# A perceiver-style block of four attention layers: the third layer's MLP in high and low parts

## The chip, the cores and the metric

The kernel runs on one core of one Trainium2 chip (trn2). The core has five engines that run their own queues of instructions in order: TensorE (PE in the profile; PEld is its weight load), VectorE (DVE), ScalarE (ACT), GpSimd (POOL) and SyncE (SP), which issues most DMAs. They meet through semaphores. The metric is the device time in microseconds (us); the number that counts is the median of several executions.

## The reference, cut to what matters

`x` has 8 batches of 256 rows of 256 values, `ctx_2048` 8 x 64 rows. Four layers follow one another, each on the whole output of the last; all arithmetic is fp32.

```python
x = _L0_xattn_ref(x, ctx, mask, ...)   # norm of ctx, 16 heads of 16, gated residual
x = _L1_xattn_ref(x, ctx, mask, ...)   # 32 heads of 8, 8 groups, residual, then a norm
x = _L2_xattn_ref(x, ctx, mask, ...)   # below: attention and MLP
x = _L3_xattn_ref(x, ctx, ctx, ...)    # two attentions with 16 heads of 128, then an MLP

def _L2_xattn_ref(...):                # the third layer
    ...                                # norm, q, k, v, softmax over 64 keys, 16 heads
    hidden = out + residual            # out @ cproj_w + cproj_b
    residual = hidden
    y = layer_norm(hidden, ln2_w, ln2_b)
    y = jax.nn.gelu(y @ fc_w + fc_b, approximate=True)   # 256 -> 1024
    y = y @ proj_w + proj_b                              # 1024 -> 256
    return residual + y
```

In the fourth layer the keys get a bias row and the MLP uses the exact gelu; before it, `kh = kv_in @ wk + bk` and `vh = kv_in @ wv + bv` project the context.

## The kernel before, in words

**Units.** The first three layers' attentions are cut into 24 units, one for each layer and batch (`NU` = 24; u = 0 to 7, 8 to 15 and 16 to 23). A unit of the third layer has two tiles of 128 rows. Each engine's program is one loop over u with a row of calls in fixed order, written out by hand; iteration u holds several units' stages: the scores of unit u, the source and queries of units u + 2 and u + 1, and the output of unit u - 1. Iteration 24 closes the last unit. Nothing is scheduled dynamically: an engine stands at a wait until it is met.

**TensorE** in an iteration of the third layer: scores of the first tile (L537), `source` (four transposes of the normed input, L421), values and keys, transposes of the previous unit's late tile (`probs_transposed`, L546), scores of the second tile, `reciprocals_transposed` (L560), `weighted` (L579), transposes of this unit's first tile, queries, `output` (L595). In iteration u, `source` needs the norm of unit u + 2 from ScalarE, and its bank is free when VectorE's `unit_residual` has added the output of unit u - 2, which stands at the head of VectorE's iteration u.

**VectorE**: `unit_residual` (L1076), sums and reciprocals of the unit before (L1050, L1057), maximum (L1028), shift (L1044) and statistics (L962, L966) of a tile, `unit_normal` (L1063), `tile_sums` (L1050). **ScalarE**: exponentials and the transposed tiles' copies (L1495, L1502), `unit_queries` (L1434), and last in the iteration the norm of a coming unit (`ln_finish`, L1484). **GpSimd**: `key_diagonal` (L1757), `reciprocals_spread` (L1769), `unit_bias` (L1797) and, for each tile, `tile_sums` (L1779, L1782), which folds the exponentials into halves and quarters for VectorE's sum; `rstd` (L1738, L1741) raises a variance to -1/2 for a norm.

**The third layer's MLP** comes behind the loop, in blocks b = 0 to 7 (one batch each). On TensorE: `mlp_source` (four transposes of the normed block), `hidden` (four banks f of 2 x 2 fp32 matmuls 128x256, L709), `projected` (16 matmuls, L722), where two banks of block b stand ahead of `projected(b - 1)` and two behind it. ScalarE applies bias and gelu (L1613). VectorE does the norm (`mlp_norm`), the affine out of PSUM (`mlp_source`, L978), the residual (`mlp_residual`, L1198); GpSimd `rstd` and the bias row on `x` (`add_row`, L1791). Between them VectorE prepares the fourth layer's weights: `wq_sums` (L1221), `wq_biased` (L1235) and `value_sums`.

**Parts.** The fourth layer's MLP is computed in products of parts already. An fp32 value is split into a high part, ScalarE's copy into the type fp32r, and a low part, VectorE's subtraction of it. `products` issues three matmuls of parts (high x high, high x low, low x high; L899 to L901) for one of fp32. The weights are split with `weight_high` (L1679) and `weight_low` (L1342), the source and the hidden values in every block (`hidden_low`, L1391; `last_hidden` on ScalarE, L1720).

**Memory and loads.** `w3` holds the small layers' weights and then four regions of the fourth layer's (queries, keys, values, output projection); `pair[0]` and `pair[1]` hold the context, the third layer's MLP weights (`w_fc`, `w_pr`) and hidden buffers. SyncE loads the fourth layer's weights (`load_w3`, L396) once the last unit's residual is done. **The fourth layer's start**: steps j from -4 on; `key_projection` (16 matmuls, L745) waits at i = 0 for the last MLP residual, at i = 1 for a bank.

## Time and profile before

| what | value |
|---|---|
| median of 3 runs (lowest, highest) | 1135.33 us (1134.01, 1136.47) |
| the profiled execution | 1134.86 us, span 1133.1 us |
| mean granted TensorE clock, share of full speed | 0.982 |
| TensorE busy | 1050.7 us, 93% |
| VectorE, ScalarE, GpSimd busy | 56%, 43%, 35% |
| chain that ended last | PE 79%, ACT 7%, POOL 7%, issue 4%, DVE 3% |
| DMA over the span | 27 GB/s |
| fourth layer's value weights | 8 DMAs of 512.0 KB, 7.7 us from issue to landing |

The span is the profiled part of one execution; the busy share of an engine is its busy time over the span. The chain is followed back from the last instruction, at each step to what released it. Rows below have the form: line in the kernel, engine, operation, output<-inputs, shape, count, and in brackets the idle time before it with what ended it. TensorE's fp32 matmuls leave two records each.

### The profile page before, as it was taken

To read this page: it belongs to the slowest core of one execution; us is meant where nothing else is said; L and a number is where in the kernel's file an instruction comes from. 1 tells how busy PE (TensorE), PEld (TensorE's weight loads), DVE (VectorE), ACT (ScalarE), POOL (GpSimd) and SP (SyncE) were. 2 spreads that over 40 slices of the span, in tenths; PEclk is the share of its full clock that TensorE was granted. 3 is DMA by queue.
4 is the path that set the end of the run, shared out by engine and by line. 5 is a ranking of instruction groups with operands and counts; after the bars stand their busy time and mean duration, and the time that the engine had idled before them with its cause. 6 is when DMAs were issued, how large, how long until landed. Compare 5 with 4: busy or idle time off the path is not lost.

```text
span 1133.1 us, 17012 instructions
## 1 busy us (share of the span) xinstructions
PE 1050.7 (93%) x6780; PEld 814.2 (72%) x6780; DVE 629.5 (56%) x1079; ACT 491.6 (43%) x988; POOL 400.5 (35%) x416
## 2 busy tenths in 40 slices
PE   6999889887899799989999999999999999978997
PEld 3666555555576688878777777777777777648997
DVE  3657888778577323732444555765444445473552
ACT  2556777676676222214333333233332333224543
POOL 2534578688975312310222212332111221231230
PEclk9999999998999999999999999999999999988999
DMA  9000000000000620000000022310000001000000
GB/s 309 33 2 1 1 1 1 1 1 1 1 1 1 223 93 1 1 1 1 1 1 1 1 75 79 108 38 1 1 1 1 1 1 64 12 0 1 29 20 29
DMA packets 17043, 32.22 MB, mean 28 GB/s; under 512 B 3522, under 2 KB 8388, under 8 KB 16452
## 3 DMA queue, kind: packets, MB, share of 16 engines
q1 hardware_dynamic: 16964, 31.13, 8.0%
q8 instruction: 54, 0.88, 0.3%
q14 instruction: 25, 0.20, 0.1%
HBM read 29.03 MB, written 2.10 MB: 27 GB/s over the span
## 4 chain that ended last, share of the span: by engine, by line
PE 79%; ACT 7%; POOL 7%; issue 4%; DVE 3%; DMA 0%; POOLq 0%; DVEq 0%; ACTq 0%
PE work L745 10%; PE work L857 10%; PE scores L796 9%; PE work L813 5%; PE scores L709 5%; PE work L722 5%; PE work L846 4%; PE work L546 4%; PE work L503 3%; PE work L595 3%; PE work L421 2%; PE work L579 2%; PE scores L537 2%; PE work L828 2%; POOL pair L1779 2%
## 5 line engine op out<-in xcount | busy, mean ns | idle before, releaser
L857 PE MATMUL work<-pair,probsT 128*128 128x256 f32 x512 | 123.5, 396 | 11.0 <-ACT pair L1658 8.8
L857 PEld LDWEIGHTS work<-pair,probsT 128*128 128x128 f32 x512 | 97.9, 196 | 36.3 <-issue 20.3
L1738 POOL TENSOR_SCALAR stat<-stat 128x2 f32<-128x2 f32 (+1 forms) x49 | 11.2, 228 | 318.4 <-DVE stat L966 317.1
L745 PE MATMUL work<-ctxT,w 128*128 128x128 f32 x1024 | 120.2, 275 | 3.5 <-ACT pair L1649 1.6
L745 PEld LDWEIGHTS work<-ctxT,w 128*128 128x128 f32 x1024 | 118.2, 192 | 5.2 <-issue 3.1
L796 PE MATMUL scores<-pair,act_bufs 128*128 128x512 f32 x256 | 115.2, 592 | 0.0
L1649 ACT ACTIVATE pair<-work 128x512 f32<-128x512 f32 x64 | 38.2, 598 | 154.3 <-PE work L813 154.3
L1639 ACT ACTIVATE kvT<-work,cols 128x128 f32<-128x128 f32 x128 | 36.6, 369 | 154.5 <-PE work L745 154.5
L1880 POOL TENSOR_TENSOR probs<-probs,smax 128x1024 f32<-128x1024 f32 x22 | 42.0, 1909 | 159.2 <-DVE smax L1314 159.2
L1294 DVE TENSOR_REDUCE smax<-scores 128x16 f32<-128x1024 f32 x32 | 39.2, 1225 | 77.1 <-PE scores L796 77.1
L796 PEld LDWEIGHTS scores<-pair,act_bufs 128*128 128x128 f32 x256 | 46.4, 190 | 46.0 <-issue 45.9
L1285 DVE TENSOR_TENSOR kvT<-work,cols 128x512 f32<-128x512 f32 x32 | 22.1, 691 | 94.0 <-PE work L745 94.0
L813 PEld LDWEIGHTS work<-kvT,w 128*128 128x128 f32 x512 | 61.9, 192 | 16.4 <-issue 16.4
L1028 DVE TENSOR_REDUCE smax<-scores 128x16 f32<-128x1024 f32 x48 | 57.8, 1205 | 21.4 <-PE scores L537 20.8
L1613 ACT ACTIVATE pair<-scores,cols 128x256 f32<-128x256 f32 x64 | 26.9, 471 | 88.6 <-PE scores L709 88.6
L813 PE MATMUL work<-kvT,w 128*128 128x128 f32 x512 | 62.5, 275 | 2.6 <-ACT kvT L1639 2.6
L846 PE MATMUL work<-w,kvT 128*64 128x256 f32 x512 | 62.3, 385 | 0.0
L722 PE MATMUL work<-pair 128*128 128x256 f32 x256 | 56.7, 379 | 0.9 <-ACT pair L1613 0.9
L546 PEld LDWEIGHTS work<-ident,pair 128*128 128x128 f32 x256 | 29.4, 148 | 38.1 <-ACT pair L1495 27.2
L546 PE MATMUL work<-ident,pair 128*128 128x128 f32 x256 | 37.3, 292 | 20.0 <-ACT w L1502 11.9
L722 PEld LDWEIGHTS work<-pair 128*128 128x128 f32 x256 | 48.6, 190 | 7.9 <-ACT pair L1613 1.3
L1791 POOL TENSOR_TENSOR x<-x,rows_late 128x512 f32<-128x512 f32 x32 | 49.7, 1552 | 12.5 <-DVE act_bufs L972 9.9
(174 smaller groups left out, 2398.3 us busy)
## 6 DMA issues: line engine op xcount, KB each, us to landing
w<-in_l_wk SPq DMA_DIRECT2D x8, 512.0 KB, 6.3
w<-in_l_wq SPq DMA_DIRECT2D x8, 512.0 KB, 7.0
w<-in_l_wv SPq DMA_DIRECT2D x8, 512.0 KB, 7.7
w<-in_l_wo SPq DMA_DIRECT2D x8, 512.0 KB, 8.4
out<-x SPq DMA_DIRECT2D x8, 256.0 KB, 2.2
x<-in_x SPq DMA_DIRECT2D x1, 1536.0 KB, 9.2
pair<-in_l_fc SPq DMA_DIRECT2D x1, 1024.0 KB, 7.2
pair<-in_l_pr SPq DMA_DIRECT2D x1, 1024.0 KB, 9.2
```

The costliest lines, as they stand in the source:

```text
L546: last = tr(work[half][:, q * P:(q + 1) * P], probs[k % 4][:, (4 * half + q) * P:(4 * half + q + 1) * P], ident[:, :])
L709: last = mm(fbank[f][:, j * T:(j + 1) * T], w_fc[:, c, (2 * f + j) * P:(2 * f + j + 1) * P], srcT[(NU + b) % 3][:, c, :], start=(c == 0), ...
L722: last = mm(work[b % 2][:, t * D:(t + 1) * D], hid_bufs[b % 2][:, f, t * P:(t + 1) * P], w_pr[:, f, :], start=(f == 0), stop=(f == FC - 1))
L745: last = mm(bank[:, h * P:(h + 1) * P], w[:, c, (4 * g + h) * K3:(4 * g + h + 1) * K3], ctxT[:, c, p * P:(p + 1) * P], start=(c == 0), sto ...
L796: last = mm(sc[j % 2][:, half * BANK:(half + 1) * BANK], fixed[j // 2 % 2][:, c, t * P:(t + 1) * P], pk[n % 2][:, bb, c, half * BANK:(half ...
L813: last = mm(step_banks(j)[2 + c][:, h * P:(h + 1) * P], w3_wq[:, 4 * g + h, c * P:(c + 1) * P], kvT[i % 2][:, h, :], start=True, stop=True)
L846: last = mm(bank[h * S:(h + 1) * S, bb * D:(bb + 1) * D], kvT[2][:, 2 * q + h, bb * S:(bb + 1) * S], w3_wo[:, 4 * g + 2 * q + h, :], start ...
L857: last = mm(step_banks(j + 1)[0][:, 0:D], probsT_bufs[j % 2][:, q, :], pv[n % 2][:, bb, q, :], start=(q == 0), stop=(q == GH // 2 - 1))
L1028: v.tensor_reduce(smax[k % 2][:, 0:GH], s3, X, ALU.max).then_inc(d_max, 1)
L1294: v.tensor_reduce(m, s3, X, ALU.max).then_inc(d_lmax, 1)
L1791: g.tensor_tensor(xb(b), xb(b), row(name).unsqueeze(1).broadcast_to([P, TT, D]), ALU.add).then_inc(done, 1)
L1880: g.tensor_tensor(pr, pr, smax[j % 2][:, 32:48].unsqueeze(2).broadcast_to([P, H3, S]), ALU.mult).then_inc(p_pr, 1)
```

## The change

The third layer's MLP goes over to three products of parts. Its weights are split in pieces (`mlp_pieces`), one in each of the iterations u = 17 to 24: the high part at the end of ScalarE's iteration, the low one near the end of VectorE's. Statistics, norm, `rstd` and bias row of blocks 0 to 2 move from behind the loop into iterations 21 to 23, the block's source into iteration 24, and `hidden(0, 0)` too, ahead of the last unit's `output`. In each block VectorE now makes the low part of the source and four low parts of the hidden values, ScalarE their high parts. `mlp_norm` of a block runs three blocks ahead instead of two. The parts need room: the fourth layer's value weights move to the first region of `w3`, and are loaded when the MLP's last product is done. The fourth layer's second key projection follows the first one directly, in a bank of the scores.

```diff
-        w_fc, w_pr = cut(DC, F), cut(FC, D)
+        mlp_raw = cut(2, DC * F)
...
-        w3_wq = w3[:, 0:WN].rearrange("p (h d) -> p h d", h=H3)
+        w3_wv = w3[:, 0:WN].rearrange("p (c n) -> p c n", c=DC)
...
+        m2_w1 = parts_at("m2_w1", w3_at, DC, F, step=pair_at[1] - w3_at)
+        m2_w2 = parts_at("m2_w2", w3_at + n_w, FC, D, step=pair_at[1] - w3_at)
+        m2_hid = [parts_at(f"m2_hid{i}", pair_at[0] + 2 * i * n_hid, FC, T) for i in range(2)]
...
+        def key_bank(i):
+            return fbank[0] if i == 1 else step_banks(i - 4)[0]
...
+        def mlp_pieces(u):
+            return {17: [0], 18: [1], 19: [2], 20: [3], 21: [4], 22: [5], 23: [6], 24: [7]}.get(u, [])
...
-                load_w3(1, g, "kqvo")
+                load_w3(1, g, "kqo")
+            e.wait_ge(pe_f2, B)
+            for g in range(4):
+                load_w3(1, g, "v")
...
+            def products(bank, stationary, moving, start, stop):
+                (s_hi, s_lo), (m_hi, m_lo) = stationary, moving
+                mm(bank, s_hi, m_hi, start=start, stop=False)
+                mm(bank, s_hi, m_lo, start=False, stop=False)
+                return mm(bank, s_lo, m_hi, start=False, stop=stop)
+            def mlp_source(b):
+                e.wait_ge(*NORMS["m2", b])
+                if b == 0:
+                    e.wait_ge(d_seen, NK)
+                elif b == 1:
+                    e.wait_ge(a_rT, NU)
+                elif b == 2:
+                    e.wait_ge(d_res, NU)
+                else:
+                    e.wait_ge(d_mT, 2 * (b - 2) + 2)
+                transposes(fbank[3] if b == 0 else work[2 + b % 2], norm[(B + b) % 3]).then_inc(pe_mx, 1)
+            def hidden(b, f):
+                e.wait_ge(a_sh, b + 1)
+                e.wait_ge(d_sl, b + 1)
+                e.wait_ge(a_wh, 4)
+                e.wait_ge(d_wl, 4)
...
+                for j in range(2):
+                    for c in range(DC):
+                        last = products(fbank[f][:, j * T:(j + 1) * T],
+                                        [w[:, c, (2 * f + j) * P:(2 * f + j + 1) * P] for w in m2_w1],
+                                        [v[:, c, :] for v in m2_src[b % 2]], c == 0, c == DC - 1)
+                last.then_inc(pe_f1, 1)
+            def projected(b):
+                e.wait_ge(a_hh, 4 * b + 4)
+                e.wait_ge(d_hl, 4 * b + 4)
+                e.wait_ge(a_wh, 8)
+                e.wait_ge(d_wl, 8)
...
+                        last = products(work[b % 2][:, t * D:(t + 1) * D],
+                                        [v[:, f, t * P:(t + 1) * P] for v in m2_hid[b % 2]],
+                                        [w[:, f, :] for w in m2_w2], f == 0, f == FC - 1)
+                last.then_inc(pe_f2, 1)
...
+                    if u == NU:
+                        mlp_source(0)
                     for k in late:
                         probs_transposed(k)
...
                     if u > 0:
                         reciprocals_transposed(u - 1)
                         weighted(u - 1)
+                    if u == NU:
+                        hidden(0, 0)
...
                 if u > 0:
                     output(u - 1)
...
-                        last = mm(fbank[f][:, j * T:(j + 1) * T], w_fc[:, c, (2 * f + j) * P:(2 * f + j + 1) * P],
-                                  srcT[(NU + b) % 3][:, c, :], start=(c == 0), stop=(c == DC - 1))
...
-            mlp_source(0, False)
-            for b in range(B + 1):
+            for f in range(1, 4):
+                hidden(0, f)
+                if f == 1:
+                    mlp_source(1)
+            for b in range(1, B + 1):
...
+                if i == 1:
+                    e.wait_ge(a_g, 4 * B)
+                else:
+                    first_free(j)
+                project(w3_wk, i, key_bank(i)).then_inc(pe_kp, 1)
...
-                if key is not None:
+                if key is not None and key != 1:
                     key_projection(j, key)
+                if key == 0:
+                    key_projection(j + 1, 1)
...
+            def mlp_stats(b):
+                e.wait_ge(d_res, 2 * B + b + 1)
+                ln_stats(("m2", b), xb(b), TT)
+            def mlp_norm(b):
...
+                ln_finish(("m2", b), xb(b), norm[(B + b) % 3], TT)
+            def mlp_weight_low(q):
+                w, q = divmod(q, 4)
+                n = mlp_raw.shape[2] // 4
+                high, low = (flat(v)[:, q * n:(q + 1) * n] for v in (m2_w1, m2_w2)[w])
+                e.wait_ge(a_wh, 4 * w + q + 1)
+                v.tensor_tensor(low, mlp_raw[:, w, q * n:(q + 1) * n], high.bitcast(F32), ALU.subtract).then_inc(d_wl, 1)
+            def mlp_source(b):
...
+                affine(fbank[3] if b == 0 else work[2 + b % 2], srcT[i % 3], "l2_g2", "l2_b2", d_mT)
+                e.wait_ge(a_sh, b + 1)
+                e.wait_ge(d_mT, 2 * b + 2)
+                v.tensor_tensor(m2_src[b % 2][1], srcT[i % 3], m2_src[b % 2][0].bitcast(F32), ALU.subtract).then_inc(d_sl, 1)
+            def mlp_hidden_low(b, f):
+                e.wait_ge(a_hh, 4 * b + f + 1)
+                high, low = (p[:, 2 * f:2 * f + 2, :] for p in m2_hid[b % 2])
+                v.tensor_tensor(low, m2_whole[f], high.bitcast(F32), ALU.subtract).then_inc(d_hl, 1)
...
+                if NU - 3 <= u < NU:
+                    mlp_stats(u - NU + 3)
+                for q in mlp_pieces(u):
+                    mlp_weight_low(q)
+                if NU - 3 <= u < NU:
+                    mlp_norm(u - NU + 3)
...
-            mlp_norm(0)
-            mlp_source(0)
-            mlp_norm(1)
             for b in range(B + 1):
+                for f in range(2):
+                    if b < B:
+                        mlp_hidden_low(b, f)
+                if b + 1 < B:
+                    mlp_source(b + 1)
                 if b > 0:
                     mlp_residual(b - 1)
-                if b + 1 < B:
-                    mlp_source(b + 1)
-                if b + 2 < B:
-                    mlp_norm(b + 2)
+                for f in range(2, 4):
+                    if b < B:
+                        mlp_hidden_low(b, f)
+                if b + 3 < B:
+                    mlp_stats(b + 3)
+                    mlp_norm(b + 3)
...
+            def mlp_weight_high(q):
+                w, q = divmod(q, 4)
+                n = mlp_raw.shape[2] // 4
+                e.wait_ge(s_in["l2_fc" if w == 0 else "l2_pr"], 16)
+                e.wait_ge(pe_wo, 2 * B)
+                act(flat((m2_w1, m2_w2)[w][0])[:, q * n:(q + 1) * n], mlp_raw[:, w, q * n:(q + 1) * n],
+                    ACT.Copy).then_inc(a_wh, 1)
+            def mlp_source_high(b):
+                e.wait_ge(d_mT, 2 * b + 2)
+                if b < 2:
+                    e.wait_ge(pe_rT, NU)
+                    e.wait_ge(d_rec, NU)
+                else:
+                    e.wait_ge(pe_f1, 4 * (b - 2) + 4)
+                    e.wait_ge(d_sl, b - 1)
+                act(m2_src[b % 2][0], srcT[(NU + b) % 3], ACT.Copy).then_inc(a_sh, 1)
...
+                for q in mlp_pieces(u):
+                    mlp_weight_high(q)
...
+            def mlp_hidden(b, f):
                 e.wait_ge(pe_f1, 4 * b + f + 1)
...
+                for j in range(2):
+                    last = act(m2_whole[f][:, j, :], fbank[f][:, j * T:(j + 1) * T], ACT.Gelu_apprx_tanh,
+                               bias=col("l2_fcb", 2 * f + j))
+                last.then_inc(a_g, 1)
+                e.wait_ge(a_g, 4 * b + f + 1)
+                if b >= 2:
                     e.wait_ge(pe_f2, b - 1)
-                for j in range(2):
-                    last = act(hid_bufs[b % 2][:, 2 * f + j, :], fbank[f][:, j * T:(j + 1) * T], ACT.Gelu_apprx_tanh,
-                               bias=col("l2_fcb", 2 * f + j))
-                last.then_inc(a_h, 1)
+                act(m2_hid[b % 2][0][:, 2 * f:2 * f + 2, :], m2_whole[f], ACT.Copy).then_inc(a_hh, 1)
...
+            def mlp_bias(b):
+                e.wait_ge(*NORMS["m2", b])
+                e.wait_ge(s_in["rows_late"], 16)
+                add_row(b, "l2_pb", p_xm)
...
+                if NU - 3 <= u < NU:
+                    rstd(("m2", u - NU + 3), TT)
+                    mlp_bias(u - NU + 3)
...
-            for b in range(B):
+            for b in range(3, B):
                 rstd(("m2", b), TT)
-                e.wait_ge(*NORMS["m2", b])
-                add_row(b, "l2_pb", p_xm)
-                if b >= 6:
-                    wq_scaled(1, b - 6)
-            wq_scaled(1, 2)
-            wq_scaled(1, 3)
+                mlp_bias(b)
+            for q in range(4):
+                wq_scaled(1, q)
```

The name of a buffer in the rows that follow is shortened by the listing (`m_w_high` is a part of the MLP's weights, `m_src_high` one of its source; `w` and `pair` are the two large regions).

**GpSimd, iterations 21 and 22**, from the second tile of unit 20 on. Before:

```order
L1779 TENSOR_TENSOR pair<-pair 128x512
L1782 TENSOR_TENSOR pair<-pair 128x256
L1779 TENSOR_TENSOR pair<-pair 128x512
L1782 TENSOR_TENSOR pair<-pair 128x256
L1769 COPY pair<-recs 128x512
L1791 TENSOR_TENSOR x<-x,pair 128x512
```

After:

```order
L1882 TENSOR_TENSOR pair<-pair 128x512
L1885 TENSOR_TENSOR pair<-pair 128x256
L1841 TENSOR_SCALAR stat<-stat 128x2
L1844 TENSOR_TENSOR stat<-stat,minus_half 128x2
L1894 TENSOR_TENSOR x<-x,rows_late 128x512
L1882 TENSOR_TENSOR pair<-pair 128x512
L1885 TENSOR_TENSOR pair<-pair 128x256
L1872 COPY pair<-recs 128x512
L1894 TENSOR_TENSOR x<-x,pair 128x512
```

Between the two `tile_sums` (one pair of rows L1779, L1782 for each tile) now stand `rstd` and the bias row of MLP block 0, which is the row ending in `rows_late`; the same stands in iterations 22 and 23.

**VectorE, the end of an iteration** (in 16 to 18), `unit_normal`, `tile_sums`, and the next iteration's `unit_residual`. Before:

```order
L1063 TENSOR_TENSOR pair<-work,pair 128x512
L1050 TENSOR_REDUCE sums<-pair 128x16
L1076 TENSOR_TENSOR x<-work,x 128x512
L1050 TENSOR_REDUCE sums<-pair 128x16
L1057 RECIPROCAL recs<-sums 128x32
L1028 TENSOR_REDUCE smax<-scores 128x16
```

After:

```order
L1104 TENSOR_TENSOR pair<-work,pair 128x512
L1091 TENSOR_REDUCE sums<-pair 128x16
L1160 TENSOR_TENSOR m_w_low<-pair,m_w_high 128x512
L1117 TENSOR_TENSOR x<-work,x 128x512
L1091 TENSOR_REDUCE sums<-pair 128x16
L1098 RECIPROCAL recs<-sums 128x32
L1069 TENSOR_REDUCE smax<-scores 128x16
```

The subtraction of a weight piece stands ahead of the residual `x<-work,x`.

**TensorE, the last unit and the MLP's start.** Before:

```order
L546 MATMUL work<-ident,pair 128x128 x8
L560 MATMUL work<-ident,pair 128x128 x4
L579 MATMUL work<-w,pair 32x256 x8
L595 MATMUL work<-w,pair 128x256 x4
L421 MATMUL work<-ident,pair 128x128 x4
L709 MATMUL scores<-act_bufs,pair 128x256 x8
L421 MATMUL work<-ident,act_bufs 128x128 x4
```

After:

```order
L609 MATMUL work<-w,pair 128x256 x4
L435 MATMUL scores<-ident,pair 128x128 x4
L560 MATMUL work<-ident,pair 128x128 x8
L574 MATMUL work<-ident,pair 128x128 x4
L593 MATMUL work<-w,pair 32x256 x8
L630 MATMUL scores<-m_src_high,m_w_high 128x256
L631 MATMUL scores<-m_src_low,m_w_high 128x256
L632 MATMUL scores<-m_src_high,m_w_low 128x256
```

The source's transposes stood behind the last `output` (L595); now they stand ahead of the last late tile's transposes (L435 after), and the first bank of `hidden` follows `weighted` (L593) directly.

## Rows read from the trace of the kernel before

**Rows 1.** Stretches of all engines: start:end, length, busy us per engine, clock, DMA, GB/s.

```profile
255.00:270.00 15.00, 11.62 (x82) 7.72 (x80) 14.69 (x24) 10.87 (x21) 12.37 (x15) 0.89 0.01 1
345.00:360.00 15.00, 15.00 (x118) 11.19 (x111) 9.74 (x13) 9.45 (x17) 8.61 (x9) 1.00 0.00 0
```

**Rows 2.** Timeline of TensorE, third layer's MLP: start, length (us), the instruction.

```profile
382.09 5.32 PE L709 MATMUL scores<-act_bufs,pair 128*128 128x256 f32 x16 [1.09 <-DVE act_bufs L978]
...
491.56 7.17 PE L722 MATMUL work<-pair 128*128 128x256 f32 x32 [0.93 <-ACT pair L1613]
```

**Rows 3.** Timeline, fourth layer's MLP.

```profile
1036.44 0.36 PE L899 MATMUL scores<-src_high,w_high 128*128 128x256 f32 x1 [1.35 <-ACT src_high L1704]
...
1057.74 1.00 DVE L978 TENSOR_SCALAR act_bufs<-work,cols 128x256 f32<-128x256 f32 x2 [2.81 <-PE work L421]
...
1062.22 0.69 DVE L1391 TENSOR_TENSOR hid_low<-w,hid_high 128x512 fp32r<-128x512 f32 x1 [0.70 <-ACT hid_high L1720]
...
1069.69 1.00 DVE L978 TENSOR_SCALAR act_bufs<-work,cols 128x256 f32<-128x256 f32 x2 [2.81 <-PE work L421]
...
1129.78 0.69 DVE L1198 TENSOR_TENSOR x<-work,x 128x512 f32<-128x512 f32 x1 [7.62 <-PE work L901]
```

**Rows 4.** Timeline, the last unit.

```profile
368.60 1.27 POOL L1779 TENSOR_TENSOR pair<-pair 128x512 f32<-128x512 f32 x1 [0.67 <-ACT pair L1495]
...
372.25 0.66 PE L560 MATMUL work<-ident,pair 128*128 128x128 f32 x4 [1.75 <-POOL pair L1769]
```

**Rows 5.** Timeline of VectorE, the weights' sums in the third layer's MLP.

```profile
487.82 1.22 DVE L1221 TENSOR_TENSOR w<-w,pair 128x1024 f32<-128x1024 f32 x1
...
490.58 4.01 DVE L1235 SCALAR_TENSOR_TENSOR pair<-w,cols,pair 128x256 f32<-128x256 f32 x4
```

**Rows 6.** Timeline, the fourth layer's weights split.

```profile
998.56 1.13 ACT L1679 ACTIVATE w_high<-w 128x512 fp32r<-128x512 f32 x2
...
1000.49 1.90 POOL L1880 TENSOR_TENSOR probs<-probs,smax 128x1024 f32<-128x1024 f32 x1 [11.94 <-DVE smax L1314]
...
1000.60 4.01 DVE L1342 TENSOR_TENSOR w_low<-w,w_high 128x512 fp32r<-128x512 f32 x2
```

**Rows 7.** Timeline, two boundaries of units, around TensorE's source transposes.

```profile
307.23 0.63 PE L421 MATMUL work<-ident,act_bufs 128*128 128x128 f32 x4 [1.57 <-ACT act_bufs L1484]
...
338.31 1.08 ACT L1484 ACTIVATE act_bufs<-x,stat 128x256 f32<-128x256 f32 x2
...
339.31 0.69 DVE L1076 TENSOR_TENSOR x<-work,x 128x512 f32<-128x512 f32 x1 [2.65 <-PE work L595]
...
339.63 1.04 POOL L1757 TENSOR_TENSOR w<-w,pair 128x512 f32<-128x512 f32 x1
...
340.38 0.66 PE L421 MATMUL work<-ident,act_bufs 128*128 128x128 f32 x4
```

**Rows 8.** Timeline, third layer's MLP, a block's norm and bias row.

```profile
388.80 0.74 DVE L962 BATCH_NORM_STATS2 stat<-x 128x6 f32<-128x256 f32 x2
...
391.72 1.27 POOL L1791 TENSOR_TENSOR x<-x,rows_late 128x512 f32<-128x512 f32 x1 [0.85 <-DVE act_bufs L972]
```

**Rows 9.** Timeline, the end of iteration 21 and the next one's start.

```profile
348.64 0.84 ACT L1434 ACTIVATE pair<-work,cols 128x256 f32<-128x256 f32 x2
...
348.65 1.28 POOL L1779 TENSOR_TENSOR pair<-pair 128x512 f32<-128x512 f32 x1 [1.69 <-ACT pair L1495]
...
351.69 1.16 DVE L1028 TENSOR_REDUCE smax<-scores 128x16 f32<-128x1024 f32 x1
...
354.14 1.06 ACT L1495 ACTIVATE probs<-probs 128x1024 f32<-128x1024 f32 x1
...
356.26 1.09 PE L546 MATMUL work<-ident,probs 128*128 128x128 f32 x8
```

**Rows 10.** Timeline of TensorE, first and third key projection of the fourth layer.

```profile
499.61 2.02 PE L745 MATMUL work<-ctxT,w 128*128 128x128 f32 x16 [0.88 <-DVE x L1198]
...
511.91 3.81 PE L745 MATMUL work<-ctxT,w 128*128 128x128 f32 x32 [0.78 <-ACT pair L1649]
```

198 lines of the change are left out of this document (86 added, 112 removed).

## The prediction

> **What bounds the kernel now.** I first read the page: TensorE is busy 93% of the span, no other engine over 56%, and the chain of work that ended last is TensorE's to 79%. An average hides stages, so I then read stretches. Around 345 to 360 us, in the later units of the third layer, TensorE is busy all 15.00 us while VectorE, ScalarE and GpSimd have 5 to 6 us free each; around 255 to 270 us it is busy only 11.62 [rows 1]. Then the timeline of the MLP that is changed. Here TensorE works without a gap from 382.09 us to 498.73: 32 records of fp32 128x256 take 7.17 us, and each full matmul leaves two records, so one costs some 0.43 us [rows 2]. Last, the fourth layer's MLP, which already does the same arithmetic in high and low parts, as a ruler: a block every 1069.69 - 1057.74 = 11.95 us for 96 products and 4 transposes (0.12 us a product, 0.36 for three) and, from its second block's first product at 1036.44 to the last residual at 1129.78, 93.3 us [rows 3].
>
> I count the units as the loop does, u = 16 to 23 for the third layer, and "iteration 24" closes it.
>
> **1. The MLP itself.** Removed: 256 fp32 matmuls; added: 768 products. Before, from the last unit's transposed reciprocals (372.25) to the MLP's first matmul are 9.84 us, and to its end 116.6 more: 126.5 in all [rows 2, 4]. After: the source's affine lies ready, so behind those reciprocals come ScalarE's copy out, its high part, VectorE's low part, some 2.6 us; then on TensorE 48 products (5.8), the last unit's output, which now stands among them (2.0), and transposes (0.4). TensorE has just idled, and before the first 16 records took 5.32 us where 32 take 7.17 [rows 2]: 1.7 to 1.9 us of slow start, which I keep. The second block waits about 1.4 for its low source, since the first residual and first hidden parts stand ahead of it. That is 14.0 us, then the ruler's 93.3.
>
> VectorE has more to do here than in the fourth layer's MLP. From the start of `wq_biased` to the end of `value_sums` are 494.59 - 487.82 = 6.8 us [rows 5], once a block in the last four blocks. In the ruler VectorE's chain from affine (1057.74) to the end of the block's last low part (1062.22, 0.69 long) is 5.1 us, as it waits for ScalarE in between, and two low parts (1.3) come before the next affine [rows 3]. With the 6.8 this is 13.2 us against TensorE's 11.95. In block 4 the 5.6 (no `wq_biased`) come on top of block 7's norm, with GpSimd's row held against it: the affine comes 3.7 us late, 0.4 of it slack. The next block adds 1.2. So 3.3 + 1.2 = 4.6 us. Sum: 14.0 + 93.3 + 4.6 = 111.9 against 126.5: **-14.6**. Bounds: without any VectorE lateness -19.2; with all of blocks 1 to 7 paced by VectorE at 13.2 to 13.6, -7.5.
>
> The Trainium skill ("FP8 and Floating Point Precision", TensorE Precision Notes) counts true fp32 as four passes, high by high, high by low, low by high and low by low. By passes alone three products would take 3/4 of the time, 0.32 instead of 0.36, and the MLP would save another 256 x 0.04 = 10 us. The ruler's row gives 0.12 a product [rows 3], and I go by it.
>
> **2. Splitting the weights in units 17 to 24.** Eight copies on ScalarE, two take 1.13 us, and eight subtractions on VectorE. Two of these, with both inputs in SBUF, take 4.01 us where GpSimd works at 1000.49, instead of 1.3: the first one finds GpSimd's 1.90 us running and ends after it [rows 6]. Busy time is no argument against them, VectorE has 5 us free; their place is. ScalarE copies at the end of its unit, and VectorE's subtraction, at the end of its own, waits for that copy; behind it in VectorE's queue stands `unit_residual`, and for this TensorE's `source` waits. Before, at 339.31: ScalarE's norm ends at 339.39, the residual runs at once, TensorE transposes at 340.38 [rows 7]. After: copy to 340.0, then GpSimd's `key_diagonal` (339.63, 1.04 us) is in the way to 340.7, subtraction to 341.3, residual to 341.95, transposes at 342.0: 1.6 us late, TensorE having nothing else in its queue. So at the starts of iterations 19, 20, 21: 3 x 1.6. At the start of 18 the norm itself is late (TensorE waits 1.57 us for it and starts at 307.23) and the same sequence ends at 309.25: 2.0 [rows 7]. Later units have no source. Sum **+6.8**. TensorE is full there, so nothing gives it back. Bounds: 3.0 (0.5 to 1.0 each, if ScalarE comes earlier), 9.
>
> **3. Norms and rows of blocks 0 to 2 in units 21 to 23.** They leave the stretch after the last unit (counted in 1) and pay at the end of each unit. The price is on GpSimd: its queue now has `rstd` and `mlp_bias`, with `tile_sums` of the unit's second tile behind them. `mlp_bias` waits for VectorE's norm, this for the subtraction, this for ScalarE's copy, this for `unit_queries` (to 349.48). From the statistics to GpSimd's row are 391.72 - 388.80 = 2.9 us where nothing is between [rows 8]. In unit 21 the statistics are done before the copy, which ends at 350.05; subtraction to 350.7, norm to 351.35, row to 352.75 [rows 9]. `tile_sums` starts then, not at 348.65, 4.1 us late. From it to the reciprocals' transposes are 3.65 us (368.60 to 372.25), and maximum, shift and exponentials take 3.5 (351.69 to 355.20) from a start 2.8 after it [rows 4, 9]: exponentials end at 359.0, transposes at 359.05 instead of 356.26. **2.8** for this unit. Played through in the same way, unit 22 adds 3.8 (its first-tile transposes come 6.6 late) and unit 23 another 3.7, since each time the second `tile_sums` stands behind three waits of other engines: the last reciprocals come 10.3 us later than at 372.25: **+10.3**. Bounds: 4 (the row costs its 1.27 alone, three times) and 13.
>
> **4. The end of the MLP and the fourth layer's start.** `value_sums` of group 3 stands ahead of the last residual: it starts some 0.8 late and the first key projection waits for it: **+0.8**. The second key projection now follows the first directly, in a scores bank. Before, from the first (499.61) to the third (511.91) are 12.3 us, TensorE waiting for ScalarE between the products [rows 10]; now the first key bias hides beside the second projection, about 10.4: **-1.9** (0 to -2.5). The values' weights are issued when the MLP's last product is done, four DMAs; they are wanted 12 us later. I cost them at nothing; that cover is gone if 512 KB took over 12 us.
>
> Everything later moves as a whole.
>
> **Sum:** -14.6 + 6.8 + 10.3 + 0.8 - 1.9 = +1.4 us. The profiled execution took 1134.86 (span 1133.1), so 1136.3; the median of the runs shown is 0.5 above that execution: **1136.7 us**. A measurement of this kernel tells 0.2%, 2.3 us, from no change: the bounds are 1133.1 and 1137.6.
>
> **Rivals.**
> A. The waits at the units' ends are mostly hidden. For it: all three engines have over 4 us free per 15 [rows 1], and a shift in one unit can be caught by another. Against: in iterations 19 to 21 TensorE has no gap to catch it with. Price: term 2 at 3.4, term 3 at 7, VectorE's lateness at 2.6: -16.6 + 3.4 + 7 + 0.8 - 1.9 = -7.3, 1128.0 us.
> B. VectorE paces the whole MLP. Place: `hidden_low` and `mlp_source` on its queue. It decides as soon as its work and its waits for ScalarE pass 11.95 us in a block; with statistics and norm (2.9 with the wait for GpSimd), four low parts and the source it is at 9.2 already without the weights' sums, so one more us in a handoff of each kind would do it. Price: the upper bound of term 1, +7.1 on my sum: 1143.8 us. A low clock in units 22 to 24 works in the same direction: at 255 to 270 us, busy 11.62 of 15, the granted clock is 0.89 [rows 1], and these units fall to a like share. The skill ("TensorE: Matmul & The Clock Gate", The HAM clock gate) says that the throttled state is the default and activity lifts it, which speaks against this change; 0 to 3 us by the row.
> C. Three of four passes. By the passes' rule (named in 1) the MLP saves another 10 us: 1126.5. The row at 0.12 us speaks against it.
>
> **Chances.** My forecast 0.34 (own range 1133.5 to 1140), A 0.31, B 0.33, C 0.02. Of my forecast's 0.34 about 0.25 lies within 0.2%, 0.02 below and 0.07 above. Faster 0.31 + 0.02 + 0.02 = 0.35, same 0.25, slower 0.33 + 0.07 = 0.40. Range 1127 to 1144: it takes in A's and B's centres.
>
> **What would show it.** In the changed profile: (1) TensorE 0.12 us apart in the third layer's MLP, blocks at 11.95 us early, 13 or more in blocks 5 and 6, with VectorE without gaps; (2) TensorE's four source transposes of units 20 to 23 each waiting 1.5 to 2 us for VectorE's residual, and subtractions of 1.2 us or more; (3) GpSimd's first `tile_sums` of a new unit 4 us after its exponentials in 22 to 24; (4) third key projection some 10.4 us after the first. I am wrong if the last unit ends less than 10 us later than before, or if the MLP's blocks stay at 11.95 throughout.

## The result: 0.36% slower, and where the profile after shows it

| | before | after |
|---|---|---|
| median of 20 executions | 1135.21 us (1133.97 to 1137.16) | 1139.34 us (1136.14 to 1143.41) |
| ratio, 95% interval | | 1.0036 (1.0023 to 1.0048) |
| profiled execution | 1134.86 us, span 1133.1 | 1136.14 us, span 1134.0 |
| mean granted clock | 0.982 | 0.979 |
| TensorE busy | 1050.7 us, 93% | 1035.2 us, 91% |

The forecast was 1136.7 us. The 20 times after fall into two groups, ten of 1136.1 to 1138.6 us with a mean clock of 0.979 to 0.974 and ten of 1140.1 to 1143.4 with 0.973 to 0.971. The profiled execution is the fastest of all. So between the two profiled executions stand 1.3 us of the 4.1; the rest goes together with a lower mean clock, to which the experiments come back.

TensorE in the profile after, at the places of [rows 2, 4, 7, 10] (start, length, instruction, idle time before it and its releaser):

```profile
309.71 0.66 PE L435 MATMUL work<-ident,act_bufs 128*128 128x128 f32 x4 [3.51 <-DVE x L1117]
...
323.84 0.66 PE L435 MATMUL work<-ident,pair 128*128 128x128 f32 x4 [1.42 <-DVE x L1117]
...
348.95 0.66 PE L435 MATMUL work<-ident,act_bufs 128*128 128x128 f32 x4 [1.42 <-DVE x L1117]
...
391.43 0.66 PE L574 MATMUL work<-ident,pair 128*128 128x128 f32 x4 [3.66 <-POOL pair L1872]
...
394.06 0.36 PE L630 MATMUL scores<-m_src_high,m_w_high 128*128 128x256 f32 x1 [0.98 <-ACT m_src_high L1609]
...
406.78 0.55 PE L630 MATMUL scores<-m_src_high,m_w_high 128*128 128x256 f32 x1 [4.58 <-ACT m_src_high L1609]
...
464.72 0.60 PE L435 MATMUL work<-ident,pair 128*128 128x128 f32 x4
...
481.64 0.60 PE L435 MATMUL work<-ident,act_bufs 128*128 128x128 f32 x4
...
507.25 2.02 PE L774 MATMUL work<-ctxT,w 128*128 128x128 f32 x16 [0.87 <-DVE x L1264]
509.11 1.95 PE L774 MATMUL scores<-ctxT,w 128*128 128x128 f32 x16
...
517.46 3.81 PE L774 MATMUL work<-ctxT,w 128*128 128x128 f32 x32 [0.78 <-ACT pair L1752]
```

The first three rows, and one at 336.40 us with 1.43 that is left out, are the last four source transposes: they wait for VectorE's residual. The reciprocals' transposes of the last unit stand at 391.43 us where they stood at 372.25, the first key projection at 507.25 instead of 499.61, the third at 517.46 instead of 511.91. As a ledger: +19.2 before the MLP, -11.5 in it, -2.1 in the key projections, so +5.55 at the third key projection; from there to the end 616.54 us instead of 621.19, -4.65, though the instructions there are the same.

The same two stretches as in [rows 1], and one in the MLP (start:end, length, busy PE, PEld, DVE, ACT, POOL, granted clock, DMA share, GB/s):

```profile
255.00:270.00 15.00, 11.60 (x80) 7.09 (x77) 14.31 (x23) 10.23 (x20) 12.46 (x14) 0.89 0.00 0
345.00:360.00 15.00, 13.58 (x101) 9.56 (x99) 10.50 (x18) 9.61 (x19) 7.51 (x9) 1.00 0.01 1
...
469.00:481.00 12.00, 9.56 (x67) 9.59 (x68) 10.40 (x21) 6.29 (x13) 2.58 (x1) 0.86 0.00 1
```

TensorE, full at 345 to 360 us before, now has 1.4 us of gaps there, and in the MLP a stretch with 2.4 us of gaps and the clock at 0.86: part of it ran at the lower level, 1.2 GHz, after TensorE had waited 3.25 us (until 471.44).

### The profile page after: what moved, and what is told of

The parts are those of the page before. It is cut to its first block, busy times and chain, and to the rows that moved or that the text cites. A ratio compares the mean times of both kernels' runs of the same rounds, so it can differ in the third digit from the quotient of the medians.

```text
span 1134.0 us, 17672 instructions
## 1 busy us (share of the span) xinstructions
PE 1035.2 (91%) x7036; PEld 811.9 (72%) x7036; DVE 662.4 (58%) x1127; ACT 518.1 (46%) x1036; POOL 403.4 (36%) x416
## 4 chain that ended last, share of the span: by engine, by line
PE 72%; ACT 8%; POOL 8%; DVE 6%; issue 5%; DMA 1%; POOLq 0%; DVEq 0%; ACTq 0%
PE work L774 10%; PE work L890 10%; PE scores L829 9%; PE work L846 5%; PE work L879 4%; PE work L560 3%; PE work L630 3%; PE work L631 3%; PE work L632 3%; PE work L517 2%; PE scores L630 2%; PE scores L631 2%; PE scores L632 2%; POOL pair L1882 2%; PE work L435 2%
## 5 line engine op out<-in xcount | busy, mean ns | idle before, releaser
L890 PE MATMUL work<-pair,probsT 128*128 128x256 f32 x512 | 120.3, 388 | 11.0 <-ACT pair L1761 8.8
L1572 ACT ACTIVATE w<-work 128x512 f32<-128x512 f32 x88 | 47.7, 593 | 14.3 <-PE work L560 14.2
L1013 DVE TENSOR_SCALAR act_bufs<-x,stat 128x256 f32<-128x256 f32 x58 | 43.2, 787 | 14.9 <-POOL stat L1844 14.9
L1882 POOL TENSOR_TENSOR pair<-probs 128x512 f32<-128x512 f32 x32 | 40.8, 1276 | 29.4 <-ACT probs L1565 29.2
```

Of the source, the lines that this page charges most:

```text
L890: last = mm(step_banks(j + 1)[0][:, 0:D], probsT_bufs[j % 2][:, q, :], pv[n % 2][:, bb, q, :], start=(q == 0), stop=(q == GH // 2 - 1))
L1882: g.tensor_tensor(halves, e3[:, :, 0:n], e3[:, :, n:S], ALU.add).then_inc(p_half, 1)
```

## The experiments

The theory after reading both traces: the loss lies in VectorE's residual behind the weight pieces, GpSimd's rows ahead of its tile sums and, not forecast, a wait for a DMA in VectorE's queue; the first gives most. The rival: these waits take each other's place, and what decides the time is how often TensorE falls to its lower clock.

All ratios and intervals are against the kernel before on the same chip (its medians there lie between 1135.0 and 1136.0 us). Since clock and noise move single executions, each kernel's profile is also read at three places. These hold noise too: after, a1, a3 and b4 run the same code up to the last reciprocals and have them at 390.2 to 393.5 us, so a difference of under 3 us in the first two columns says little by itself.

| kernel | last reciprocals | third key projection | from there to the end | median, ratio (95%) |
|---|---|---|---|---|
| before | 372.25 | 511.91 | 621.19 | 1135.21 |
| after | 391.43 | 517.46 | 616.54 | 1139.34, 1.0036 (1.0023 to 1.0048) |
| a1, after again | 390.37 | 517.89 | 616.91 | 1136.73, 1.0014 (1.0004 to 1.0023) |
| a2 | 382.44 | 508.58 | 616.62 | 1132.19, 0.9971 (0.9949 to 0.9993) |
| a3 | 390.22 | 514.47 | 616.43 | 1134.89, 1.0000 (0.9990 to 1.0009) |
| a4 | 386.05 | 514.48 | 621.12 | 1137.73, 1.0017 (1.0007 to 1.0027) |
| b1 | 378.89 | 503.16 | 616.84 | 1121.15, 0.9871 (0.9856 to 0.9885) |
| b2 | 380.47 | 504.01 | 616.99 | 1125.65, 0.9908 (0.9891 to 0.9925) |
| b3 | 374.52 | 511.96 | 616.44 | 1129.07, 0.9938 (0.9921 to 0.9955) |
| b4 | 393.50 | 517.56 | 620.84 | 1137.90, 1.0021 (1.0009 to 1.0033) |
| c1 | 373.23 | 518.33 | 619.37 | 1139.10, 1.0029 (1.0018 to 1.0041) |
| c2 | 372.21 | 513.53 | 619.27 | 1135.56, 1.0004 (0.9994 to 1.0013) |
| c3 | 378.07 | 498.31 | 616.79 | 1121.96, 0.9893 (0.9846 to 0.9939) |
| d1 | 374.26 | 496.14 | 616.76 | 1114.71, 0.9815 (0.9801 to 0.9828) |

**a1_again.** No edit.

> The changed kernel, unchanged. Its 20 executions lie in two groups, 1136.1 to 1138.6 us with a mean granted clock of 0.974 to 0.979 and 1140.1 to 1143.4 with 0.971 to 0.973, while the 20 of the kernel before lie within 1134.0 to 1137.2. Theory: the upper group is the same program with one or two more stretches at the lower clock, in the third layer's MLP or the units before it, where TensorE now idles more. Rival: the stretch lies in the fourth layer, where nothing was changed, and is chance. The profile shows in which stretches the granted clock is under 1; both theories expect about 1139 us and the same two groups.

Measured: 1136.73 us, all ten executions between 1135.9 and 1138.4 (0.979 to 0.974), so the upper group did not come on this chip, and no profile of the changed kernel holds it. The first theory placed the second group in the MLP and the units, the rival in the fourth layer; this run decides nothing.

**a2_low_behind_residual.** VectorE's subtractions of the weight pieces (`mlp_weight_low`) go behind the next iteration's residual:

```diff
                     tile_shifted(*tiles[0])
...
+                for q in mlp_pieces(u - 1):
+                    mlp_weight_low(q)
...
-                for q in mlp_pieces(u):
-                    mlp_weight_low(q)
```

> VectorE's subtraction of a weight piece goes behind the next iteration's residual and first tile's shift; nothing is left out. Theory: TensorE's waits of 1.4 us for the residual at the source transposes of iterations 19, 20 and 21 and 1.9 of the 3.5 in 18 vanish, and in 21 to 23 the norm no longer stands behind the subtraction and its wait for ScalarE's copy, so GpSimd's row comes 1 to 2 us earlier: last unit's transposed reciprocals 7 to 10 us earlier than 391.4 us, time 6 to 8 us less than the changed kernel. Rival: the subtraction at the new place delays the exponentials by as much, and 0 to 2 us are left.

Measured: the four waits are gone (the source transposes of iteration 18 wait 1.55 us for ScalarE's norm, as before), last reciprocals 7.9 us earlier than in a1, third key projection 9.3. The lowest executions took 1127.2 us against 1135.9; five of ten lie at 1135.0 to 1135.6 with 0.973 to 0.974, so the median fell by 4.5 only, where 6 to 8 were expected. The theory holds for the mechanism and for its price on the path. One part of it does not: the norms no longer stand behind the subtraction, but from the source transposes of unit 23 to the last reciprocals it still takes 42.18 us (42.78 in a1), so GpSimd's row gained nothing to speak of.

**a3_rows_later.**

```diff
-            e.wait_ge(s_in["ln_rows"], 16)
-            for a in range(2):
...
             for b in range(B + 1):
...
+                if b == 1:
+                    e.wait_ge(s_in["ln_rows"], 16)
...
```

> The difference of the fourth layer's norm rows, for which VectorE stands at a DMA until 402.4 us in the changed kernel, goes from ahead of the MLP's first low parts to behind block 1; nothing is left out. Theory: the wait of 4.6 us for the second block's source falls to 1.4 and the time by 3 us. Rival: VectorE, which paces the last blocks with the weights' sums, gives the gain back there: under 1 us.

Measured: the wait falls from 4.54 us to 2.67, the third key projection comes 3.4 us earlier, the lowest execution is 1133.1 against 1135.9, the median 1.8 less. This was the theory, but for the wait, which was to fall to 1.4: 2.67 us are not the DMA's. The row of after that gave the theory is VectorE's, idle for a DMA with the first low parts behind it:

```profile
402.42 0.76 DVE L1306 TENSOR_TENSOR pair<-pair 128x256 f32<-128x256 f32 x2 [4.23 <-DMA pair<-in_ln_rows]
403.10 1.29 DVE L1177 TENSOR_TENSOR m_hid_low<-pair,m_hid_high 128x512 fp32r<-128x512 f32 x2
```

**a4_bias_later.** GpSimd's `mlp_bias(b)` one iteration back, behind `tile_sums(tiles[0][0])`:

```diff
+                if NU - 3 < u <= NU:
+                    mlp_bias(u - NU + 2)
...
                     rstd(("m2", u - NU + 3), TT)
-                    mlp_bias(u - NU + 3)
```

> GpSimd's bias rows of blocks 0 to 2 go one iteration back, behind the tile sums of the next iteration, so that no tile sum stands behind a row that waits for ScalarE's copy, VectorE's subtraction and its norm; rstd stays. Theory (the row's waits cost 10.3 us by the end of the last unit): last reciprocals 7 to 9 us earlier, time 6 to 9 us less. Rival: the row costs only its 1.27 us three times, which stay: under 3 us.

Measured: last reciprocals 4.3 us earlier than in a1, third key projection 3.4; the median is not lower (1137.73), because from there to the end it took 621.12 us instead of 616.91. On the path that is half of the expected 7 to 9 us, between the theory and the rival (under 3); in the median nothing is left of it.

**b1_three_moves.** The three edits together.

> The three moves of the first set together: the subtraction behind the residual, the rows' difference behind block 1, GpSimd's bias rows one iteration back. Fast executions so far: 1136.0 us unchanged, 1127.2, 1133.1 and 1133.6 with one move each. Theory: each removes a wait of its own, but the first took part of the row's wait already (norms no longer stand behind the subtraction), so 8.8 + 2.9 + 1 to 2: fast executions at 1122 to 1124 us, last reciprocals at about 378 us. Rival: what the moves give, the clock takes back, since TensorE stands idle in the same places: a spread of 8 us between executions as with the first move alone, and a median not under 1130.

Measured: 1121.15 us, 15.6 less than a1 and 1.3% under the kernel before; lowest 1120.5; last reciprocals 378.89. The rival said not under 1130 and falls. At the third key projection the three moves add up: 9.3, 3.4 and 3.4 us one by one, 14.7 together. The medians do not (4.5 and 1.8 less, 1.0 more), since the single moves' executions spread over the clock and these four do not.

**b2_sums_spread, b4_spread_alone.** In the kernel before, L1221 is `wq_biased` and L1235 `value_sums` (`wq_sums` stands ahead of them). Of these sums, the value heads go two at a time ahead of the source's affine, on b1 and on the changed kernel:

```diff
+                if 1 <= b < B:
+                    value_heads(1, 2 * b - 2, 2 * b)
                 if b + 1 < B:
                     mlp_source(b + 1)
...
-                    value_sums(1, b - 4)
+                if b == B:
+                    value_heads(1, 14, 16)
```

> As b1_three_moves, and of the fourth layer's weights' sums the 16 value heads go two at a time into blocks 1 to 8 of the MLP, ahead of the source's affine, where VectorE idles 2.8 us at 450.6 in the changed kernel, instead of four at a time in blocks 4 to 7. Theory (VectorE paces blocks 4 to 7: 16.9, 13.3 and 13.0 us instead of 11.95): all blocks at 12 to 12.4, 5 to 6 us less than b1. Rival: the affine is now late in every block, since 2.0 us of heads run against GpSimd's row on the shared port or against ScalarE: each of seven blocks 0.5 to 1 us longer, and no gain.

> The changed kernel with the value heads' spreading of b2 alone. Theory: the block of 16.9 us and the two of 13 go, 5 to 6 us less than the changed kernel's 1136.0 in fast executions, and fewer low-clock stretches at 470 and 495 us, since TensorE no longer idles there: the slow group goes down too. Rival: under 2 us less, as the lateness is ScalarE's (its hidden parts) and not the sums'.

Measured: no gain in the time of either: b2's median is 4.5 us above b1's, b4's 1137.90 lies between the changed kernel's two, 1136.73 and 1139.34. The early blocks stay at 11.95 us, so the rival of b2 (every block longer) is wrong too. The long block takes 16.20 us (451.92 to 468.12) in b2 and 14.70 in b4, where b1 and the changed kernel have 16.92. TensorE's wait in it is 2.52 us in both, where it was 3.25: spreading the heads took 0.7 off. The rest of the difference is the clock, 0.71 behind this wait in b2 (460 to 464 us) and 1.00 in b4. What holds the wait at 2.52, is in b2's timeline:

```profile
451.13 3.48 DVE L1177 TENSOR_TENSOR m_hid_low<-pair,m_hid_high 128x512 fp32r<-128x512 f32 x2
451.29 2.77 POOL L1978 TENSOR_TENSOR w<-w,pair 128x1024 f32<-128x1024 f32 x1 [1.19 <-DVE pair L1279]
```

GpSimd's scaling of the query weights starts as soon as the first query sums are done, and two low parts that take 1.29 us alone take 3.48 beside it. In this block stand the last norm, the first query sums and that collision; the value heads alone did not make it long. The Trainium skill ("Trainium Architecture — The Big Picture", What this means for kernel authors) calls the port that VectorE and GpSimd share an exclusive lock. The rows agree in the main: the two low parts end 0.55 us behind GpSimd's instruction (454.61 against 454.06), as if the second had run only after it, though 3.48 is less than the sum of 1.29 and 2.77.

**c3_sums_behind_norms.** As b1, but three heads a block in 1 to 4, one in 5 to 8, and the query sums from block 5 on, where no norm stands; the last of them (`wq_biased(1, 2)`, `wq_sums(1, 3)`, not shown) stand ahead of the MLP's last residual:

```diff
+                if 1 <= b <= 4:
+                    value_heads(1, 3 * b - 3, 3 * b)
...
-                if 4 <= b < 8:
-                    wq_sums(1, b - 4)
+                if 5 <= b < B:
+                    wq_sums(1, b - 5)
```

> As b1_three_moves (1121.2 us), with the weights' sums placed by what VectorE has free: three value heads in each of blocks 1 to 4 ahead of the affine, one in each of 5 to 8, and the query weights' sums one block later, 5 to 8, so that GpSimd's scaling (2.77 us) no longer runs against the first block's two low parts (3.48 us instead of 1.29 in b2's profile) behind block 7's norm. Theory: the block of 16.9 us goes to 12.5 and the one of 13.3 too, 4 to 5 us less: 1116.5 us. Rival: the collision with GpSimd only moves to another block and two thirds of the 5 us stay: 1119 to 1121 us.

Measured: every block from the third on at 11.95 to 12.08 us, third key projection 4.85 us earlier than in b1, two executions at 1117.1 (b1: 1120.5 at the same clock of 0.983). The other two lie at 1126.8 with 0.976, so the medians of b1 and c3 can't be told apart. The place was right, the gain is on the path. It has a price of its own: `wq_biased` waits 2.48 us for GpSimd's scaling with the last residual behind it, and the first key projection waits 1.67 us for that residual instead of 0.87.

**b3_key_alone.** The kernel before with the second key projection alone moved.

```diff
+                if key == 0:
+                    key_projection(j + 1, 1)
```

> The kernel before with the second key projection alone moved behind the first, into a bank of the scores. Theory: 1.9 us less (12.3 us from the first to the third become 10.4; the changed kernel's profile has 10.2). Rival: the value projection waits instead and nothing is left: 0 to 0.5 us.

Measured: -6.5 us. From the first to the third projection 10.21 us instead of 12.30, as expected; for the other 4.4 us no theory was on record. **c1 and c2** put TensorE work in at that point of the kernel before:

```diff
+                for _ in range(3 if i == 0 else 0):
+                    project(w3_wk, i, step_banks(j)[0])
                 project(w3_wk, i, step_banks(j)[0]).then_inc(pe_kp, 1)
```

> The kernel before, with the fourth layer's first key projection issued four times into the same bank instead of once: 3 x 1.9 = 5.6 us more TensorE work at 499.6 us, everything behind it that much later, as in the changed kernel's profile. There the fourth layer, from the third key projection on, took 616.5 us instead of 621.2. Theory (which stretches before the last MLP fall to the lower clock, 985 and 1010 to 1030 us here, hangs on when they come, not on this change): the time rises by clearly less than 5.6 us, about 1 us, at a mean clock of 0.985. Rival: those stretches belong to the fourth layer's own waits: the time rises by 5.6 us, at 0.982.

> As c1_before_plus_5_6 with one repetition: 1.9 us more work. The key projection alone (b3) gave 6.5 us where 2.1 leave the stretch from the first to the third projection, and its profile has the lower clock only at 1010 to 1020 us. Theory: moving by 2 us either way can change which stretches fall: the time does not rise by 1.9 but by something between -3 and +6, with the clock moved the same way. Rival: 1.9 us, at 0.982; then the 4.5 us of b3 are of its own doing.

Measured: +4.0 us for 5.6 added (interval 2.0 to 4.7) and +0.5 for 1.9 (-0.7 to 1.5). In their profiles the first to the third projection takes 5.4 and 1.8 us longer, and what follows 1.8 and 1.9 less. The theory of c1 said about +1 and was too bold; that what follows is no constant, it had right, and more work does not shift the time by as much. c2's theory (anything from -3 to +6) was too wide to be tested; its rival, 1.9 us at 0.982, lies just outside the interval.

The strongest evidence is in the table. From the third key projection on these kernels run the same instructions, and they need 616.4 to 617.0, 619.3 or 620.8 to 621.2 us. The kernel before and b3 reach that projection within 0.05 us of one another. Before, and then b3 (stretches as above):

```profile
980.00:1000.00 20.00, 16.98 (x76) 11.90 (x75) 9.96 (x16) 7.36 (x12) 1.90 (x1) 0.91 0.00 1
1000.00:1020.00 20.00, 12.47 (x47) 8.66 (x46) 16.14 (x27) 4.39 (x7) 8.77 (x9) 0.84 0.00 0
1020.00:1040.00 20.00, 16.12 (x98) 14.87 (x97) 7.36 (x15) 9.78 (x19) 1.09 (x1) 0.82 0.00 1
```

```profile
980.00:1000.00 20.00, 16.98 (x79) 11.45 (x78) 11.55 (x19) 7.36 (x12) 3.04 (x2) 1.00 0.00 1
1000.00:1020.00 20.00, 12.46 (x49) 9.38 (x48) 14.55 (x24) 4.39 (x7) 8.73 (x9) 0.83 0.00 0
1020.00:1040.00 20.00, 16.12 (x130) 15.56 (x129) 9.31 (x19) 10.86 (x21) 3.22 (x3) 1.00 0.00 1
```

TensorE is busy as long in each (16.98, 12.5, 16.12 us), but the clock is 0.91 and 0.82 in the one and 1.00 in the other, and b3 gets more done (130 matmul records instead of 98). TensorE's waits are the same too. The first one behind which the two part, before and then b3:

```profile
985.93 5.38 PE L857 MATMUL work<-pair,probsT 128*128 128x256 f32 x16 [2.28 <-ACT pair L1658]
...
985.99 3.69 PE L863 MATMUL work<-pair,probsT 128*128 128x256 f32 x16 [2.28 <-ACT pair L1666]
```

Behind the same wait of 2.28 us the same 16 records take 5.38 us in the one and 3.69 in the other. So whether the clock falls behind a wait of some us is not settled by the program from there on. It isn't plain chance either: all four executions of b3 lie at 0.985 to 0.986, and the 67 of the kernel before that ran beside the experiments at 0.979 to 0.983. The Trainium skill ("TensorE: Matmul & The Clock Gate", The HAM clock gate) says that the monitor's window runs free and does not start with the kernel; that fits one program having two groups of executions (c3: 1117.1 and 1126.8 us), and no run here shows the window itself.

The changed kernel and b4 stand in the same relation (517.46 and 517.56 us, 616.54 and 620.84 behind them). b4 from 980 us:

```profile
980.00:1000.00 20.00, 17.72 (x81) 11.89 (x80) 10.15 (x16) 5.31 (x9) 5.48 (x3) 0.91 0.00 1
1000.00:1020.00 20.00, 12.92 (x57) 9.16 (x55) 15.98 (x25) 6.39 (x10) 5.97 (x5) 0.97 0.00 1
1020.00:1040.00 20.00, 16.29 (x78) 14.39 (x79) 8.24 (x16) 6.05 (x10) 3.88 (x5) 0.69 0.00 1
```

**d1_norms_behind_reciprocals.** As c3; `rstd` behind the late tile sum of the next iteration, `mlp_norm` behind VectorE's reciprocals, and the pieces two at a time:

```diff
-            return {17: [0], 18: [1], 19: [2], 20: [3], 21: [4], 22: [5], 23: [6], 24: [7]}.get(u, [])
+            return {17: [0, 1], 18: [2, 3], 19: [4, 5], 20: [6, 7]}.get(u, [])
```

> As c3_sums_behind_norms (1117.1 us in its fast executions, 1126.9 in the others), with two more moves: rstd and norm of blocks 0 to 2 go behind the next unit's late tile sum and VectorE's reciprocals, where GpSimd idles 1.5 us, instead of ahead of them; and the weights are split two pieces an iteration in 17 to 20, not one in 17 to 24. In c3 the copy of the reciprocals on GpSimd comes every 11.8 us in iterations 22 to 24 (365.32 to 377.08), before it was 9.3 (362.31 to 371.58), and the norm takes 2.09 us as GpSimd's tile sum runs beside it. Theory (the last reciprocals, still 6 us later than in the kernel before, are late because rstd, norm and pieces stand in those two queues): the period goes to 9.5 to 10.5, the last reciprocals to 374 to 375 us, 3 to 4 us less, 1113 to 1114 in fast executions. Rival: TensorE's own order of the late tiles sets the period and the double pieces make ScalarE late in 18 to 21: no gain or 1 to 3 us more. A second group some 6 to 9 us above the first is expected by both, as the clock falls somewhere else in about half the executions.

Measured: 1114.71 us, 0.9815 of the kernel before, the fastest of all, as the theory said; no second group in five executions, which both had expected. Last reciprocals 374.26, only 2.0 us later than in the kernel before. GpSimd:

```profile
362.61 0.22 POOL L1853 TENSOR_SCALAR stat<-stat 128x2 f32<-128x2 f32 x1
362.92 0.73 POOL L1856 TENSOR_TENSOR stat<-stat,minus_half 128x2 f32<-128x2 f32 x1
363.74 0.61 POOL L1884 COPY pair<-recs 128x512 f32<-128x512 f32 x1
...
373.60 0.61 POOL L1884 COPY pair<-recs 128x512 f32<-128x512 f32 x1
```

`rstd` fills the time in which GpSimd waited for the reciprocals; the copies come 9.9 us apart, not 11.8. Which of the two moves did it was not tried apart. Some is left: the first key projection waits 3.19 us for the last residual, which again stands behind `wq_biased` and its wait for GpSimd, and then takes 3.42 us at the lower clock instead of 2.02.

## Why the prediction came out as it did

It forecast +1.4 us for the profiled execution and 1136.7; that execution took +1.3, the median +4.1. Part of the agreement is luck. At the third key projection the change costs 5.55 us where 1.4 were forecast: the source transposes of unit 23 come 1.8 us later than forecast, the rest of the units takes 0.3 more, the MLP 2.3 more, the key projections 0.2 less. That the unchanged rest then took 4.65 us less covered it. No term said so.

- **Term 2, the pieces at the units' ends: right.** Forecast 2.0 and three times 1.6; the rows show 3.51 - 1.57 = 1.94 and 1.42, 1.43, 1.42, together 6.2. The chain is the forecast one. Iteration 21 after, against [rows 7]:

```profile
346.38 0.62 ACT L1597 ACTIVATE m_w_high<-pair 128x512 fp32r<-128x512 f32 x1
...
346.71 1.04 POOL L1860 TENSOR_TENSOR w<-w,pair 128x512 f32<-128x512 f32 x1
...
347.03 1.27 DVE L1160 TENSOR_TENSOR m_w_low<-pair,m_w_high 128x512 fp32r<-128x512 f32 x1 [3.29 <-ACT m_w_high L1597]
348.22 0.68 DVE L1117 TENSOR_TENSOR x<-work,x 128x512 f32<-128x512 f32 x1
```

  The piece takes 1.27 us beside GpSimd's `key_diagonal` (0.68 alone), and the residual stands behind it. a2 took all of it back. The source transposes of unit 23 come 8.6 us late, not 6.8: behind the wait of 3.51 us TensorE runs at the lower clock from 311.5 us on (eight transposes take 1.97 us instead of 1.09), about 1.6 in all (14.13 us to the next source transposes, 12.56 in the iteration after), and 0.5 was there before the first piece. The forecast had no term for the clock here.
- **Term 3, GpSimd's rows: size right, cause partly.** Forecast 10.3; 19.18 - 8.57 = 10.6. The forecast put it on the row that waits. For the first of the three units the chain came out to 0.1 us: the transposes forecast at 359.05 stand at 367.67, which is 8.57 plus 0.05 later.

  But a4 took away just the row's wait and did not get it all back. From the source transposes of unit 23 to the last reciprocals it takes 31.87 us before, 42.48 after and 42.78 in a1, 38.04 in a4, 37.47 in b1, 32.44 in d1, where `rstd`, norm and pieces are out of those places. So somewhat over two fifths were the row's wait. The rest is held by `rstd`, norm and pieces in two queues that set the units' pace, since d1 has nearly all of it back; by which of them is not shown. One way is seen in c3: `rstd` stands ahead of the late tile sum, and the norm takes 2.09 us beside that sum instead of 0.73.
- **Term 1, the MLP: right sign, too large.** Forecast -14.6 to its end; from 391.43 to the first key projection -11.5, where with term 4's 0.8 the forecast was -13.8. Start (2.6 us) and products (0.12) as forecast. The step that failed is "the second block waits about 1.4 for its low source, since the first residual and first hidden parts stand ahead of it": what also stands ahead is the difference of the norm rows, which waits for a DMA until 402.42. The wait was 4.58. a3 shows 1.9 of it to be the DMA's; the 2.67 left are still nearly twice the forecast. The slow start of 1.8 did not come at the first bank but behind that wait: from 406.78 to the next source transposes 10.13 us, where the ruler has 8.71.

  VectorE's lateness was forecast as 4.6 us over two blocks (its terms, 3.3 and 1.2, add up to 4.5) and cost 5.0 (16.92 - 11.95), but otherwise: one affine comes 3.6 us late, as forecast (3.7), TensorE waits 3.25 for its source, and the other 1.7 are the lower clock behind that wait. The next affine waits for TensorE and is not late, where 1.2 more were forecast. The late affine, and the wait:

```profile
468.96 0.99 DVE L1019 TENSOR_SCALAR act_bufs<-work,cols 128x256 f32<-128x256 f32 x2
...
471.44 0.54 PE L630 MATMUL scores<-m_src_high,m_w_high 128*128 128x256 f32 x1 [3.25 <-ACT m_src_high L1609]
```

  From the third block on all others ran at 11.95. Rival B is refuted: VectorE paced one block in eight.
- **Term 4: the key projections right (-2.1 for -1.9), the late residual wrong.** The last residual waits 0.79 us for TensorE, not TensorE for it. The values' weights at nothing: right, no wait shows them.
- **"Everything later moves as a whole": wrong.** From the third key projection to the end the profiled execution is 4.65 us shorter, and this covers what was missed in term 1 and at 311 us.
- Rival A, waits mostly hidden, is refuted by the four source waits, C by the products at 0.12 us.
- The median's other 2.8 us: the executions of the upper group have a mean clock lower by 0.006 than those of the lower. That they are the ones with the longer last stretch (621 instead of 616.5 us), as b4 and a4 have it at 0.973 and 0.974, is likely but not shown, since no profile of this kernel holds one. It would explain 4.5 of the 5.0 us between the groups. In the kernel before, whose profile has the long form too, the 67 executions don't fall into two groups.

## What to carry to other kernels

An instruction put into a full queue costs little by its own time and much by what it waits for and what stands behind it: place it behind the instruction that the bounding engine waits for, and in the gap that its queue has anyway (b1 turned +0.4% into -1.3% and d1 into -1.9% by order alone, with every instruction kept). Look through all waits that a moved block meets on its way, DMA waits included, not only those that it brings along. And compare the profiles of two kernels at a common point ahead of unchanged code before comparing their spans.

## What the runs showed of the hardware

- The same 616 to 621 us of instructions took up to 4.75 us more in one kernel than in another, with TensorE arriving within 0.05 us, the same waits and the granted clock as the only difference found in the rows: behind the same wait of 2.28 us the same records took 5.38 us in one and 3.69 in the other. Single programs have two groups of executions 5 to 10 us apart (after: means of 1136.9 and 1141.9; c3: 1117.1 at 0.983, 1126.8 at 0.976).
- A VectorE subtraction with both inputs in SBUF takes 0.69 us alone and 1.27 beside GpSimd's 1.04; two take 1.29 alone and 3.48 beside its 2.77. A norm's two instructions took 2.09 instead of 0.73 beside GpSimd's 1.26.
